# A graph network's gather ring doubled to 32 tiles, with one landing semaphore per block and one ring of one-hots

## The reference

```python
dst = (12500 * uniform(200000) ** 2).astype(int)      # sorted by dst, src follows
def _sage_layer(x, src, dst, inv_deg, W_self, W_neigh, b):
    agg = segment_sum(x[src], dst, num_segments=12500)
    return x @ W_self + (agg * inv_deg[:, None]) @ W_neigh + b
h = relu(_sage_layer(layernorm(x), ...)); h = relu(_sage_layer(h, ...)); h = _sage_layer(h, ...)
x = x + h
# feed-forward: weights = layernorm(x) @ wr + br; the top 6249 nodes get
# (gelu(ln @ w1 + b1) @ w2 + b2) * weight added; w1 is 256x1024, w2 is 1024x256
x = x + ffn(layernorm(x))
```

## Time and profile before

| | us |
|---|---|
| median of 3 runs | 6444.89 |
| span of the profiled execution | 7838.5 |
| POOL busy in the span | 4678.4 (60%) |
| PE busy in the span | 4641.2 (59%) |
| DVE, ACT busy | 2368.1, 896.4 |
| gathers (L504) | 4704, 4576.5 busy |
| DMA engines, mean busy share of the gather queue | 42.2% |
| mean granted TensorE clock | 0.761 |

### The profile page before, as it was taken

The page is one execution under the profiler, slowest core; times in us unless marked ns, Lnnn a source line. Parts: engine busy times, 40 slices in busy tenths (PEclk is TensorE's granted clock), DMA queues, the critical chain, the costliest instruction groups (busy, mean ns, idle before and its releaser), DMA issues.

```text
span 7838.5 us, 97787 instructions
## 1 busy us (share of the span) xinstructions
PE 4641.2 (59%) x19986; PEld 2616.3 (33%) x20208; DVE 2368.1 (30%) x5119; ACT 896.4 (11%) x2129; POOL 4678.4 (60%) x4762
## 2 busy tenths in 40 slices
PE   0445556666777544555555666544556667777884
PEld 0112223333444212222222223212334445555663
DVE  7111222233333211122233333211222233344446
ACT  3000000011111000000000000000111122223331
POOL 5666666666666566666666666666655555555551
PEclk9666677777888766667777777666767788888997
DMA  5444444444454444444445544444444444444444
GB/s 197 136 135 133 134 132 137 132 139 139 140 142 140 129 138 133 140 135 138 138 137 144 143 139 142 134 136 132 131 121 117 115 118 121 119 123 121 126 125 160
DMA packets 460486, 1056.21 MB, mean 135 GB/s; under 512 B 128083, under 2 KB 234279, under 8 KB 460455
## 3 DMA queue, kind: packets, MB, share of 16 engines
q0 software_dynamic: 301056, 925.15, 42.2%
q10 hardware_dynamic: 82364, 97.08, 3.5%
q1 hardware_dynamic: 77035, 33.62, 1.6%
HBM read 971.47 MB, written 84.02 MB: 135 GB/s over the span
## 4 chain that ended last, share of the span: by engine, by line
issue 38%; PE 32%; POOL 10%; another core or an unknown queue 8%; DVE 5%; DMA 2%; DVEq 2%; ACT 1%; SPq 1%; ACTq 0%; POOLq 0%
PE agg L613 12%; POOL gath L504 9%; PE agg_lo L614 6%; PE hid L657 5%; PE y L667 4%; DMA gath<-table,idx_ring 2%; PE hid L553 1%; PE y L553 1%; DVE resid L750 1%; PE hid L578 1%; DVEq L859 1%; DVE onehot L855 1%; DVEq L855 1%; PE agg_lo L603 0%
## 5 line engine op out<-in xcount | busy, mean ns | idle before, releaser
L504 POOL DMA_INDIRECT gath<-table,idx_ring x4704 | 4576.5, 973 | 2923.2 <-issue 1362.3
L613 PE MATMUL agg<-gath,onehot 128*128 x5778 | 2633.4, 478 | 2256.1 <-issue 1759.7
L855 DVE TENSOR_TENSOR onehot<-window_ids,dst_f 128x512 f32 x1464 | 1016.1, 694 | 3949.7 <-PE agg_lo L614 1434.4
L614 PE MATMUL agg_lo<-gath,onehot 128*128 x5856 | 1935.1, 330 | 380.5 <-issue 336.1
L613 PEld LDWEIGHTS agg<-gath,onehot 128*128 x5856 | 662.6, 113 | 3493.9 <-issue 3204.3
L614 PEld LDWEIGHTS agg_lo<-gath,onehot 128*128 x5856 | 660.1, 113 | 760.6 <-issue 576.0
L657 PE MATMUL hid<-featT,w_gnn 128*128 128x128 f32 x3136 | 485.4, 306 | 278.9 <-issue 277.4
L657 PEld LDWEIGHTS hid<-featT,w_gnn 128*128 128x128 f32 x3136 | 449.3, 218 | 311.9 <-issue 306.4
L667 PE MATMUL y<-w_sb,hidT 128*128 128x256 f32 x1568 | 392.5, 408 | 13.9 <-issue 10.9
L667 PEld LDWEIGHTS y<-w_sb,hidT 128*128 128x128 f32 x1568 | 317.1, 208 | 64.0 <-issue 15.1
L1103 ACT ACTIVATE featT<-tp 128x256 f32<-128x256 f32 x196 | 74.2, 379 | 2201.3 <-remote 1540.7
(11 more groups left out here) (129 smaller groups left out, 2462.0 us busy)
## 6 DMA issues: line engine op xcount, KB each, us to landing
gath<-table,idx_ring POOLq DMA_INDIRECT x4704
table<-split ACTq DMA_DIRECT2D x194, 192.0 KB
table<-gath ACTq DMA_DIRECT2D x24, 768.0 KB, 3.6
xb<-x ACTq DMA_DIRECT2D x97, 128.0 KB
yw_dram<-yw ACTq DMA_DIRECT2D x97, 128.0 KB
resid<-x SPq DMA_DIRECT2D x24, 512.0 KB, 7.3
gath<-yw_dram SPq DMA_DIRECT2D x12, 512.0 KB, 7.7
out<-gath ACTq DMA_DIRECT2D x12, 512.0 KB, 9.1
```

Source lines behind the costliest of these rows:

```text
L504: g.indirect_dma_start(gath[:, j, 0:PARTS * D], None, table[layer][:, :], bass.IndirectOffsetOnAxis(ap=idx_ring[:, h, j:j + 1], axis=0)).t ...
L613: mm(hi_mid, oh, tile_rows[:, :, 0:2 * D], start=False, **flags)
L614: last = mm(agg_lo[p][:, 0:lo_cols], oh, tile_rows[:, :, 2 * D:2 * D + lo_cols], start=False, **flags)
L855: v.tensor_tensor(onehot[p][:, bass.ds(slot, GROUP), :], window_ids[p][:].unsqueeze(1).to_broadcast([P, GROUP, P]), dst_f[:, bass.ds(tiles ...
```

## The change

The ring `gath` gets 32 tiles, so 8 blocks. The four gathers of a block share one landing semaphore, 8 semaphores in place of 16. The two rings of one-hots become one ring of 32, whose slot is given by the count of (block, window) pairs, `b + n`; the one-hots of block b now wait until block b-7 is released. `idx_ring` keeps its two halves of 16 tiles. The rest makes room: `dst_f` is cut to 1,568 columns, `zeros` to 128 columns (so the opening product is made in two halves of 256 columns, with `ones` as its moving side), the weights of layer 2 are loaded by ScalarE (ACT) into `hidT[0]` after layer 0, the 12 `fin` buffers all lie in `gath`, and small work areas share space.

```diff
-RING = 16
+RING = 32
-    TURN_TILES = 2 * RING
+    TURN_TILES = RING
+    HALF_TILES = TURN_TILES // 2
+    HALF_BLOCKS = HALF_TILES // GROUP
-        onehot = [sb(f"onehot{p}", [P, RING, P], BF16) for p in range(2)]
+        onehot = sb("onehot", [P, RING, P], BF16)
-        idx_ring = sb("idx_ring", [P, 2, RING], I32)
+        idx_ring = sb("idx_ring", [P, 2, HALF_TILES], I32)
+        w_gnn2 = hidT[0][:].rearrange("p k n -> p (k n)").rearrange("p (k n) -> p k n", k=KD)
-        landed = [sem(f"landed{j}") for j in range(RING)]
+        landed = [sem(f"landed{q}") for q in range(RING_BLOCKS)]
...
                     for h in range(2):
-                        for j in range(RING):
-                            sp.wait_ge(landed[j], it * 32 + 16 * (2 * layer * TURNS_PER_LAYER + h + 1))
-                            if j % GROUP == GROUP - 1:
-                                sp.sem_inc(rows_ready, 1)
+                        for q in range(h * HALF_BLOCKS, (h + 1) * HALF_BLOCKS):
+                            sp.wait_ge(landed[q], it * (16 * GROUP) + 16 * GROUP * (layer * TURNS_PER_LAYER + 1))
+                            sp.sem_inc(rows_ready, 1)
...
-                        for q in range(RING_BLOCKS):
-                            pool.wait_ge(slots_free, it * (2 * RING_BLOCKS)
-                                         + (layer * PADDED_BLOCKS + h * RING_BLOCKS + q + 1))
+                        for q in range(h * HALF_BLOCKS, (h + 1) * HALF_BLOCKS):
+                            pool.wait_ge(slots_free, it * RING_BLOCKS + (layer * PADDED_BLOCKS + q + 1))
...
-                                                     ).then_inc(landed[j], 16)
+                                                     ).then_inc(landed[q], 16)
...
-                mm(hi_mid, zeros[:, 0:P], zeros[:, 0:2 * D], start=True, **free)
-                mm(agg_lo[p][:, 0:lo_cols], zeros[:, 0:P], zeros[:, 0:lo_cols], start=True, **free)
+                for h in range(2):
+                    mm(agg[p][:, h, :], zeros[:], ones_bf[:, 0:D], start=True, **free)
+                mm(agg_lo[p][:, 0:lo_cols], zeros[:], ones_bf[:, 0:lo_cols], start=True, **free)
                 def block_products(b, last_block=False):
                     base = pe.snap((b % RING_BLOCKS) * GROUP)
+                    pair = pe.snap(((b + n) % RING_BLOCKS) * GROUP)
...
-                    dve.wait_ge(slots_free, b + (layer * PADDED_BLOCKS + 1))
-                    v.tensor_tensor(onehot[p][:, bass.ds(slot, GROUP), :],
+                    dve.wait_ge(slots_free, b + (layer * PADDED_BLOCKS + 2))
+                    v.tensor_tensor(onehot[:, bass.ds(pair, GROUP), :],
...
             act.wait_ge(mm_ready, NT)
+            act.wait_ge(hT_ready, NT)
+            for h, w in enumerate((w_neigh[2], w_self[2])):
+                act.dma_start(w_gnn2[:, :, h * D:(h + 1) * D],
+                              w.rearrange("(k p) n -> p k n", p=P)).then_inc(w2g_loaded, 16)
```

More of the change, by code:

```diff
@@ L63, in gnn_ffn_program @@
     assert 3 * BLOCK_BITS < 31 and NT % 2 == 0
-    assert NT == LAST_LOOPED + 2 and BATCHES % 4 == 1 and RING == 4 * BATCH
+    assert NT == LAST_LOOPED + 2 and BATCHES % 4 == 1 and RING >= 4 * BATCH and PAIRS % RING_BLOCKS == 0
     FFN_ROUNDS = 6
@@ L137, in gnn_ffn_program @@
         fin = [area[:, k * BATCH * D:(k + 1) * BATCH * D].rearrange("p (b d) -> p b d", d=D)
[L138 to L141, removed]
+               for area, bufs in ((gath[:].rearrange("p r d -> p (r d)").bitcast(F32), FIN_BUFS),)
                for k in range(bufs)]
         assert len(fin) == FIN_BUFS
[L144 to L147, removed]
+        part, trial, gains = (stats4[0][:].rearrange("p b s -> p (b s)")[:, k * TRIALS:(k + 1) * TRIALS]
+                              for k in range(3))
+        sel = inv_deg
         agg = [psum(f"agg{p}", [P, 2, D]) for p in range(2)]
@@ L686, in total @@
                 pe.wait_ge(part_ready, i + 1)
-                mm(totals_ps, ones[:], part[:], start=True, stop=True).then_inc(total_ready, 1)
+                mm(totals_ps, ones[:, 0:P], part, start=True, stop=True).then_inc(total_ready, 1)
             last = NT - 1
@@ L851, in block_onehots @@
                 def block_onehots(b):
-                    slot, tiles = dve.snap((b % RING_BLOCKS) * GROUP), dve.snap(b * GROUP)
-                    dve.wait_ge(slots_free, b + (layer * PADDED_BLOCKS + 1))
-                    v.tensor_tensor(onehot[p][:, bass.ds(slot, GROUP), :],
+                    pair, tiles = dve.snap(((b + n) % RING_BLOCKS) * GROUP), nc.s_assert_within(
+                        dve.snap(b * GROUP), 0, (BLOCKS - 1) * GROUP,
+                        skip_runtime_bounds_check_because="blocks are counted from the sorted edges, below BLOCKS")
+                    dve.wait_ge(slots_free, b + (layer * PADDED_BLOCKS + 2))
+                    v.tensor_tensor(onehot[:, bass.ds(pair, GROUP), :],
                                     window_ids[p][:].unsqueeze(1).to_broadcast([P, GROUP, P]),
@@ L995, in _ @@
             link(v.memset(wanted, float(SELECTED)))
-            link(v.memset(part[:], 0.0))
+            link(v.memset(part, 0.0))
             totals = [0]
```

58 lines of the change are left out of this document (32 added, 26 removed).

## The result

The changed kernel takes 6458.43 us (median of 20 runs, 6452.99 to 6472.16), the kernel before 6446.01 us (median of 20, 6440.41 to 6462.33). The ratio is 1.0019 with a 95% interval of 1.0013 to 1.0026: 12 us slower. The forecast was 6370.

The account below looks back on a forecast made before the run. POOL's pace was taken to bound layers 0 and 1 and layer 2's long windows, PE the later part of layer 2. 6445 - 80 (boundary stalls) + 5 (opening product) = 6370 us; forecast 6333 to 6425, 8-in-10 range 6190 to 6458.

Parts of the forecast that it names:

- What bounds the kernel: POOL's pace of gathers bounds layers 0 and 1 and layer 2's long windows; PE bounds the later part of layer 2.
- the 1438 us of stalls: POOL's stalls with all four ring blocks held, in the profile before; taken as largely that profiled execution's own.
- The stock of 83 us: Whole kernel: real stalls the change can take, 6445 less a sum of 6362 at 1.25 us a gather.
- A stall of 1.7 us at each of the first 48 windows' ends: Layer 2: POOL stalls until PE releases the shared block; the ring of 8 blocks removes this, -80 us.
- A deeper ring only moves them: Last 50 windows of layer 2: POOL's 579.0 us of waits behind PE are moved, with no gain.
- PE's price of late slots: Layer 2: a window with t new tiles costs PE 10.5 + 0.33 t us; PE's excess over POOL is 94 us.
- The register for the pair: PE's register for the one-hots' slot: taken as 0; +14 us if 0.07 us on each of about 200 uses.
- The opening product: Made in halves, one more PE instruction per window: 0.1 us in each of 50 windows PE paces, +5 us.
- The semaphore, the weights' load, the `fin` buffers: SP's single wait per block, layer 2's weights loaded after layer 0, the last output stage: 0 each.
- The one-hots: 0, with bounds of -20 and +10: DVE's one-hots, up to 7 blocks ahead: 0 us, bounds for DVE's writes falling differently beside POOL's.
- The slower rival: Layer 2: PE's path per block lengthened by the second register computation and extra opening product, 59 us longer, 6500; chance 0.14.
- "no change" rival: Without a profile POOL never waits for a slot, its pace nearer 1.27 us: 6440, from 6433 to 6458; chance 0.18.

Follow-up runs that it names:

- the second profile: Kernel before, unchanged, profiled again: span 6460.0 us; 6466.24 us beside 6466.97 in the same session, ratio 1.000.
- the third profile: Kernel before, unchanged, profiled once more in a later session: 6443.61 us, ratio 0.9998.
- experiment 2: Changed kernel with its ring of 8 blocks, but gathers and one-hots only 4 blocks ahead: ratio 1.0019 to the kernel before.
- experiment 8: Kernel before, with PE computing the one-hots' slot again in a second register per block, same value: ratio 1.0009; changed kernel beside it 1.0015.
- experiment 6: Changed kernel again, ratio 1.002; with a second set of one-hots written in layers 0 and 1, 1.0035; with one-hots only 4 blocks ahead, 1.001.
- experiment 9: Changed kernel with two rings of one-hots by block number, 4 ahead, and one whole opening product: 6442.95 us (ratio 0.9995), then 6440.72 (0.9987).

## Why the prediction was wrong

*What bounds the kernel.* Right in kind. POOL's pace bounds layers 0 and 1, and nothing is left there to wait for. Doubtful in one reason: the 1438 us of stalls were laid to the profiled execution. On one chip the kernel takes 7719.58 us without a profile too, so such a disturbance needs none.

*The stock of 83 us.* This is the step that failed first. It was the difference between the median and a sum with 1.25 us a gather, the pace of the undisturbed row. The mean pace is 1.276 to 1.286 us, as one gather in three beside a one-hot is longer; this alone is 4704 x 0.03 = 141 us. The earlier trace rows had the mean, 973 ns, and the sum of 6400 with it left 45 us, from which the PE-bound windows had still to be paid. The prediction saw this ("at 1.278 us a gather nothing is left") and took the pace of the undisturbed row all the same, which left room for a gain. Measured in its place: 40.3 us of stalls.

*A stall of 1.7 us at each of the first 48 windows' ends.* This is the term of -80 us, and it is wrong: the second profile has 9 us of stalls in these windows, and the third 11. At most of their ends POOL doesn't stall at all. Most of the 40.3 us stand in the last windows. The single stall read off was one of the disturbed execution. That two estimates met at 80 us was no confirmation: each had a free choice in it (the pace, 1.7 between 0.7 and 3.5).

*"A deeper ring only moves them"* was said of the last windows, and is right: layer 2's gathers end 31 us earlier, and the tail is 24 us longer. The lead is worth 10 to 20 us of layer 2 and tail (table: 2227.4 against 2208 to 2211 with the change's other parts; 2211.4 for the second register against 2201.5 and 2197.9 for the two rings, which differ in more than the lead), and in the time of the whole kernel nothing that can be told (experiment 2).

*PE's price of late slots.* The slot of the earlier trace rows was taken for one of 16 tiles; its trace holds the products of 12. And it was a slot of the disturbed execution. So 10.5 + 0.33 t gives 14.5 for a slot of 16 tiles (t = 12) and 13.1 for one of 12 (t = 8), where the third profile has mostly 13.8 to 14.0 and 11.8 to 12.2. PE's excess over POOL was put at 94 us beside the stalls. Layer 2 and tail of experiment 2 are 2227.4 us; POOL's busy time, its regular gaps and a tail of 155 us make 1547.5 + 478 + 155 = 2181 of it. So PE's excess is about 46 us with all stalls in it, half of the 94.

*The register for the pair: "I take 0, as PE's registers run ahead of its products"* is the second step that failed. The trace lists the same number of register instructions, yet those ahead of the high and middle products take 626.3 us in the sum, and not 555.8: 48 ns more per use of a block. (The added register of experiment 8 takes 653.2, so 66 ns more, with the same late slots.) In PE-bound slots this shows in full: 4.2 to 4.5 us over 40 slots, and about 6 in the kernel's time by the ratio of experiment 8. The price of 0.07 us that was named as a bound was of the right size; the value taken wasn't.

*The opening product.* Put at +5; in halves the ratio is 0.9997 (0.9988 to 1.0006), so nothing that can be told.

*The semaphore, the weights' load, the `fin` buffers.* The semaphore alone shows nothing that can be told. At the start of layer 1 POOL waits 28.1 us in the changed kernel and 28.2 before, so the load is hidden. The `fin` buffers weren't tried alone.

*The one-hots: 0, with bounds of -20 and +10.* Here the larger part of the loss stands. The changed kernel's gathers carry 15 to 50 us more excess than those of the ring of 16 (161 to 171 against 121 to 146), the most in layer 1. The prediction named the way (DVE's writes falling differently beside POOL's) and gave it a bound that was too small. That a one-hot instruction begun just before a gather makes it longer is shown by the counts in experiment 6. That it is the slot by pair, and not the lead, is what the grouping in experiment 9 leaves over, by a small margin.

In sum, by the means of the table: the changed kernel's layers 0 and 1 are some 25 us longer than those of the kernel before, by the excess of their gathers, and layer 2 with the tail is some 5 us shorter, where the lead's 10 to 20 us are mostly taken back by PE's late slots and longer gathers. This makes 20 us, beside the 12 measured, within what such profiles scatter.

The slower rival named PE's path per block as its mechanism and the register as its cause. It had one part of the loss right, too large (59 us), with a chance of 0.14. The "no change" rival had the right account of POOL's pace. The measured 6458.43 us lie just beyond the wide range (6190 to 6458), but that is close only because the range had the "no change" rival in it; the forecast's own 80 us aren't there. The span expected of the profile after, 7000 to 7500 us, rested on the disturbance and came to 6470.4.

## What to carry to other kernels

A deeper ring pays for the time that the producer really waits for a slot. Count that wait first, less the regular gap, at the mean pace of the producer and not at its best; here it was 40 us of 6446, and of the 31 that the gathers of layer 2 gained 24 came back in the tail. If the profile's span is far above the median, get a second profile before reading any stall. A register computation that is added to an inner loop isn't free where the engine is the bound, even if no instruction is added. And an instruction of another engine may cost the producer by the moment at which it starts: look at which of the producer's instructions are longer than the usual one, and what began just before them.

## What was not expected of the hardware

The same kernel takes 6446 us on one chip and 7720 on another, and in a profile from there register instructions of 0.7 us stand on PE, DVE and SP, while POOL's gathers keep their usual 0.95 us. What causes it wasn't found.

A gather of 128 rows takes 0.95 us of POOL, but up to 1.47 us if a one-hot instruction of DVE began in the 0.5 us before. One that begins together with the gather or during it leaves it as it is, and 976 more such instructions added only 12 us.
